# First pooling of a graph U-Net: the turned tiles use four banks of their own, and 64 skip products move behind the half turn

## The reference, cut to what matters

```python
def topk_pool(x, w, src, dst, mask, k):
    score = jnp.tanh((x * w).sum(-1) / jnp.sqrt((w * w).sum()))
    _, idx = jax.lax.top_k(score, k)
    ...
    mask2 = mask & kept[src] & kept[dst]
    return (x[idx], new_id[src], new_id[dst], mask2, idx)
...
for i in range(DEPTH):
    x = gcn_conv(x, dn_W[i], dn_b[i], src, dst, mask, n)
    x = jax.nn.relu(bn_train(x, dn_g[i], dn_beta[i]))
    xs.append(x)
    k = int(RATIO * n)
    x2, src2, dst2, mask2, idx = topk_pool(x, pool_w[i], src, dst, mask, k)
    ...
x = jax.nn.relu(gcn_conv(x, bot_W, bot_b, src, dst, mask, n))
for i in range(DEPTH):
    ...
    x = jnp.concatenate([xf, xs[DEPTH - 1 - i]], axis=1)
    x = gcn_conv(x, up_W[i], up_b[i], src, dst, mask, n)
    x = jax.nn.relu(bn_train(x, up_g[i], up_beta[i]))
```

## Time and profile before

| | |
|---|---|
| time, median of 3 runs | 1024.85 us (1023.67 to 1025.37) |
| profiled execution, span | 1043.1 us |
| mean granted TensorE clock | 0.970 |
| PE busy | 914.4 us (88%) |
| DVE busy | 593.5 us (57%) |
| ACT busy | 404.2 us (39%) |
| POOL busy | 62.9 us (6%) |
| POOL's gathers, line 832 | 20, 945 ns each |

### The profile page before, as it was taken

One profiled execution on the slowest core, in us unless ns is written; L12 is line 12 of the kernel. 1 busy time (PEld: TensorE's weight loads), 2 busy tenths in 40 slices (PEclk: granted clock), 3 DMA queues, 4 the chain that ended last, 5 costly groups with the idle time before them and its releaser, 6 DMA issues.

```text
span 1043.1 us, 17654 instructions
## 1 busy us (share of the span) xinstructions
PE 914.4 (88%) x7259; PEld 604.6 (58%) x7259; DVE 593.5 (57%) x1559; ACT 404.2 (39%) x897; POOL 62.9 (6%) x84
## 2 busy tenths in 40 slices
PE   2348999999999999999999999686988788899997
PEld 1346666876755557766475665555545445456555
DVE  5779999996937934463230265454462555525311
ACT  0889999992652001464020031555214412221200
POOL 4000000000000000000000001322002200130000
PEclk9979999999999999999999999897999699999999
DMA  5010000006920002003000004573214100151002
GB/s 161 8 28 2 2 1 2 2 2 272 401 116 1 1 1 64 1 2 125 1 1 1 1 1 121 210 221 83 92 35 134 47 1 2 34 218 67 2 1 64
DMA packets 39359, 65.86 MB, mean 63 GB/s; under 512 B 3508, under 2 KB 27293, under 8 KB 38756
## 3 DMA queue, kind: packets, MB, share of 16 engines
q1 hardware_dynamic: 34318, 45.14, 12.5%
q0 software_dynamic: 4064, 17.86, 5.3%
q10 hardware_dynamic: 886, 1.61, 0.5%
HBM read 28.29 MB, written 36.31 MB: 62 GB/s over the span
## 4 chain that ended last, share of the span: by engine, by line
PE 59%; DVE 26%; ACT 5%; DMA 3%; issue 3%; another core or an unknown queue 3%; POOL 0%; ACTq 0%; DVEq 0%; SPq 0%; POOLq 0%
PE psum L3115 25%; DVE region L1076 7%; PE psum L2497 7%; DVE region L1069 6%; PE psum L2609 6%; PE psum L2838 3%; PE psum L2574 2%; DVE region L1674 2%; PE psum L2402 2%; PE psum L2940 2%; PE psum L2427 1%; PE psum L3062 1%; PE psum L2931 1%; ACT region L2222 1%
## 5 line engine op out<-in xcount | busy, mean ns | idle before, releaser
L3115 PE MATMUL psum<-adj,region 128*128 128x448 fp8e4 (+1 forms) x1200 | 202.6, 329 | 1.1 <-DVE region L1913 1.0
L3115 PEld LDWEIGHTS psum<-adj,region 128*128 128x128 f16 x1200 | 116.5, 98 | 81.0 <-DVE region L1913 1.7
L2427 PE MATMUL psum<-region 128*128 128x200 bf16 (+2 forms) x1176 | 111.7, 230 | 26.8 <-DVE region L1076 18.5
L2427 PEld LDWEIGHTS psum<-region 128*128 128x128 bf16 x1176 | 93.7, 99 | 61.3 <-DVE region L1076 32.9
L2064 ACT ACTIVATE adj<-psum 128x400 fp8e4<-128x400 f32 x196 | 86.4, 519 | 14.9 <-PE psum L2431 14.3
L1076 DVE TENSOR_TENSOR region<-iota_key,region 128x1200 bf16<-128x1200 bf16 x147 | 91.2, 672 | 0.0
L2402 PE MATMUL psum<-adj,region 128*128 128x448 fp8e4 x350 | 90.4, 350 | 0.0
L1674 DVE CAST region<-psum 128x512 fp8e4<-128x512 f32 (+2 forms) x87 | 47.3, 597 | 75.1 <-PE psum L2931 35.5
L1069 DVE TENSOR_TENSOR region<-iota_lo,region 128x3072 bf16<-128x3072 bf16 x49 | 85.5, 1746 | 5.9 <-PE psum L2431 5.7
L2222 ACT ACTIVATE region<-psum 128x512 fp8e4<-128x512 f32 (+6 forms) x111 | 62.0, 599 | 66.5 <-PE psum L3097 20.8
L1941 DVE SCALAR_TENSOR_TENSOR region<-psum,unfit,region 128x448 f32<-128x448 f32 (+3 forms) x34 | 20.1, 622 | 109.5 <-PE psum L3115 97.3
(11 more groups left out here) (376 smaller groups left out, 1281.3 us busy)
## 6 DMA issues: line engine op xcount, KB each, us to landing
both_table<-adj SPq DMA_DIRECT2D x1, 10000.0 KB, 28.7
adj_table<-adj SPq DMA_DIRECT2D x1, 10000.0 KB, 54.7
region<-dk_dram SPq DMA_DIRECT2D x2, 1568.0 KB, 6.3
both_table<-region SPq DMA_DIRECT2D x1, 2704.0 KB, 10.9
half_table<-region SPq DMA_DIRECT2D x2, 832.0 KB, 5.2
xs_dram<-nodebuf SPq DMA_DIRECT2D x1, 1600.0 KB, 5.2
nodebuf<-xs_dram SPq DMA_DIRECT2D x1, 1600.0 KB
half_table<-region SPq DMA_DIRECT2D x2, 768.0 KB, 5.6
```

Source lines behind the costliest of these rows:

```text
L2427: pe.matmul(psum[:, q % BUILD_BANKS, i * KEYS + k0:i * KEYS + k1], hot_lo[:, r, c, j, :, i], hot_key[:, r, c, j, k0:k1, i], start=(n == 0) ...
L3115: last = pe.matmul(psum[:, b if b < BLOCKS else LAST_BANK, 0:width], here[:, t, k, :], rows, start=(t == 0 and k == 0), stop=(t == n_src - ...
```

## The change

Three things are changed in the first pooling, and one with them in the second.

- The rings are tables: at level 0 two banks for each engine, 3 and 4 for ScalarE and 5 and 7 for VectorE; at level 1 three for each as before. The place in the ring is counted from the first unit of the pooling.
- At level 0 the 64 last products of pass 0 move from before the half turn to behind it, ahead of the 50 of pass 1, and `take_skip(0)` moves on ScalarE to just before `take_skip(1)`. Units of level 0 no longer wait for `skip_out`.
- Pass 1 sums into bank 6 in place of 7. Since the degree sums stand in bank 6 too, the first of them waits for `take_skip(1)`.
- At level 1 the first unit now uses bank 0, so it waits for the first copy of `take_skip(2)`, where it waited for the second.

```diff
-TURN_BANKS = 3
+TURN_BANKS = (((3, 4), (5, 7)), ((0, 1, 2), (3, 4, 5)))
...
-        SKIP_PASSES = ((0, 0, 3, 0), (0, 3, 4, 7), (0, 4, BLOCKS, 0), (1, 0, 3, 0), (1, 3, 4, 3))
+        SKIP_PASSES = ((0, 0, 3, 0), (0, 3, 4, 6), (0, 4, BLOCKS, 0), (1, 0, 3, 0), (1, 3, 4, 3))
...
-            bank = TURN_BANKS * e + k % TURN_BANKS
+            banks = TURN_BANKS[level][e]
+            bank = banks[u // 2 % len(banks)]
...
-                        take_skip((0, 2, 3)[below])
+                        if below > 0:
+                            take_skip((0, 2, 3)[below])
                         for u in range(0, turns(below) if below < PACKINGS else 0, 2):
                             e, k, bank, to, source = turn_unit(below, u)
                             if u in (len(half_units(below)), len(half_units(below)) + 1):
                                 if below == 0:
+                                    take_skip(0)
                                     take_skip(1)
...
-                skip_sums(skips, SKIP_PICK[below][3], skip_sizes(skips))
+                if below > 0:
+                    skip_sums(skips, SKIP_PICK[below][3], skip_sizes(skips))
+
                 def sum_degrees(n):
...
-                        if below == 1:
+                        if below == 0:
+                            pe.wait_ge(skip_out, SKIP_OUT[1])
+                        else:
                             pe.wait_ge(skip_kept, SKIP_GROUPS[1])
...
                         if below == 0:
+                            skip_sums(0, SKIP_PICK[0][3], skip_sizes(0))
                             skip_sums(1, 0, skip_sizes(1))
...
-                    if k >= TURN_BANKS and e == 0:
-                        pe.wait_ge(act_turned, k - TURN_BANKS + 1)
-                    elif k >= TURN_BANKS:
-                        pe.wait_ge(dve_turned, k - TURN_BANKS + 1)
-                    if e == 0 and u // 2 < TURN_BANKS:
-                        pe.wait_ge(skip_out, (0 if below == 0 else SKIP_OUT[1]) + bank + 1)
+                    ring = len(TURN_BANKS[below][e])
+                    if u // 2 >= ring and e == 0:
+                        pe.wait_ge(act_turned, k - ring + 1)
+                    elif u // 2 >= ring:
+                        pe.wait_ge(dve_turned, k - ring + 1)
+                    if below == 1 and e == 0 and u // 2 < ring:
+                        pe.wait_ge(skip_out, SKIP_OUT[1] + bank + 1)
```

## The result

The change made the kernel slower. Its median is 1041.11 us (1036.74 to 1041.49, 4 runs) against 1025.11 us (1023.67 to 1027.32, 4 runs) before; the ratio is 1.0143, 95% interval 1.0121 to 1.0164. Timed again beside later runs, it was 1037.70 against 1024.65 (4 and 17 runs), ratio 1.0127 (1.0110 to 1.0143); so the loss is 16.0 us by the first medians and 13.1 by the second. I had forecast 1023.9 and a range up to 1027.2.

A forecast was written before the change was run, and what follows sets the result against it. It took late signals from TensorE to copying engines under gathers as the bound. First pooling -0.8 and second -0.4 sum to -1.2 us; allowing for the clock, 1024.85 - 1.0 gave 1023.9, range 1020.2 to 1027.2.

The forecast's parts named there:

- What bounds the kernel now: First pooling: signals from TensorE to a copying engine are late while gathers flow, a handoff of 7.3 us against 0.43.
- three holes in the chain: First pooling: ScalarE waits 24.88 us, TensorE 7.97 us before the half turn, and the full turn is held until 714.8.
- Half turn, -1.4 us: First pooling: 16 matmuls filled early give -1.7 us, rings of two cost +0.3; last fill from 689.51 to 688.1.
- Skip products: First pooling: 114 products take 21.9 us, until 710.0; the moved 12.3 us lie under the store and second gathers.
- Full turn, 1.13 us a tile: First pooling: 13 tiles from 712.4 at 1.13 us (bounds 1.05 and 1.20) take 14.7 us; last degree sum at 727.3.
- Clock: First pooling: TensorE at 1.2 GHz as the half turn starts, at the high level throughout the full turn.
- D: First pooling, slower: full turn starts cold and late, unit 82 at 714.0, low clock for 5.5 us; +3.2, 1028.0; chance 0.19.
- Second pooling, -0.4 us: Second pooling: first fill needs one skip copy, not two, so copies and next gathers come sooner; bounds 0 and -0.5.
- A: First pooling: with short handoffs under gathers the half turn ends 7.5 to 8.4 us earlier; time 1016.4; chance 0.12.
- wrong for me: Sign in the new profile against the forecast: half turn's copies spread over 656 to 663.

The follow-up runs named there:

- the run with dummies: The change plus 64 dummy products, whose results nothing reads, in TensorE's idle time between the picks and the half turn; 1037.40 us, ratio 1.0127.
- the half of the move: Against the change with rings of three in the full turn: 32 of the 64 products put back ahead of the half turn; 1028.71 us, ratio 1.0044.
- both parts undone: Against the change: products back ahead of the half turn and rings of three in the full turn, rings of two in the half turn alone; 1026.54 us.

## Why the prediction was wrong

**What bounds the kernel now: here it failed.** I read three holes in the chain and built on "a signal from TensorE to a copying engine is late while gathers flow". The one trace of before had them; the second trace of the same kernel has a handoff of 0.03 us under the same gathers, and no other trace of this study has such a hole. I had put the 18.2 us between span and median beside the profile and carried differences over all the same. They weren't spread over the program, as I took for granted: 19.8 us lay in the stretch on which the whole sum stood. All terms that used it, from the start of the half turn to unit 82, compared the change with a kernel that the timed runs don't show.

**Half turn, -1.4 us.** I took the start of the fills at 655 to 656 against an old start of 664.37. The clean old start is 14.3 us after the first pick (656.15), the new one 13.3 (659.14): only 1.0 us sooner, since the data are there 659.14 - 648.21 = 10.9 us after the first gather's start, which in the clean trace is 655.2, and the products end there at 655.43. The half turn then takes 25.8 us where it took 23.8: by the run with dummies (24.8) the low clock costs about 1 us and the rings of two another, where I had +0.3 for them. So it ends no sooner: the products behind it start 684.75 - 645.86 = 38.9 us after the pick, against 679.79 - 641.90 = 37.9. The term is +1.0, not -1.4.

**Skip products.** Sized right (21.7 us; I had 21.9) and placed wrongly. "The second gathers, in which TensorE turned only three tiles" was the perturbed trace. In the clean one TensorE turned tile after tile as they landed, from 691.16 - 641.90 = 49.3 us after the pick. With 114 products it can't start before 706.31 - 645.86 = 60.5. The delay is 11.2 us of the 13.6, with the half turn's 1.0 in it; the other 2.4 are the turn's own length, 79.4 - 60.5 = 18.9 us against 707.72 - 691.16 = 16.6. I had let the moved 12.3 us cost next to nothing. The run without 58 of them shows the term by time, 8.8 us, and the run with all back ahead, 9.1.

**Full turn, 1.13 us a tile.** Measured 1.41. My round of one bank was right at 1.12, but the degree sum of 0.30 stands, in the code, behind the wait for the bank and ahead of the fill, so it belongs to the round whole: 0.60 + 0.09 + 0.30 + 0.43 = 1.42. I had read the loop and not the order of its two waits. 13 x 0.28 = 3.6 us over my term. Alone it is worth less: with the products ahead the turn waits for gathers anyway, which GpSimd issues 1.25 us apart, and the rings of two cost 2.5 us (1028.61); with rings of three the move costs 6.5 us (1031.59), as a turn that starts late finds its data landed and runs at 1.05, 718.32 - 703.57 = 14.8 us in place of 16.6; both together cost 13. Each takes the cover of the other.

**Clock.** I took the high level in the full turn, and it was 1.00 there (D's fall did not come). Low in the half turn's start, as forecast.

**Second pooling, -0.4 us.** Right in mechanism: the first fill comes 0.69 us after the skip copies' start in the change's trace (792.68 - 791.99) and 0.73 in the run with this step alone, against 1.26, so 0.57 and 0.53 us sooner, just over my bound of 0.5. No time shows it (1024.13 against 1024.65, ratio 1.0000).

**The rivals.** A's mechanism is what the trace of the change shows, prompt handoffs while the gathers flow: its turn copies run on from 659.78, the very sign that I had named as wrong for me. Against the trace that I read, the pooling did get shorter, by (728.46 - 642.88) - 79.4 = 6.2 us, where A had 8. (Its 702 for the end of the products should be 703 to 704 by my own terms; nothing hangs on that.) The Trainium skill's rule (SBUF, Who interferes with whom) that DMA never contends with a compute engine agrees with the traces in what it speaks of, the engines' own work: the 64 products take 12.27 us under the gathers in both traces of the kernel before. It names no signals; but in the second trace those too are prompt, and I set a single trace against them. But A's price was wrong by its sign: with prompt signals the kernel before has them too, and no hole of 7.97 us to close. None of my rivals asked what the change costs if before is as prompt as after. Rival D had the right side for the wrong reason.

**What stays open.** Why the first profiled execution had late signals. It was told by its span, 18 us over the median; it didn't come back in thirteen further traces, so I could not test it, and whether the signals were late or the waiting engines themselves stood is open with it. Open as well are whether the loss from partly moved products has a floor, the 3.4 us between the two medians of the change, and the other half of what rings of two cost in the half turn beside VectorE's pace.

## What to carry to other kernels

Before reading a trace, hold its span against the timed runs of the same kernel: where they differ by more than the forecast effect, find the stretch in which the excess lies, or reason from what the engines would do without it. Work that stands ahead of a wait for data is free up to the wait's length; to move it behind is free only if the next wait is as long and nothing useful was done in it. When a ring of buffers gets shorter, write down everything between the wait for a buffer and its refill, in code order: all of it is in the round, and what doesn't need the buffer belongs ahead of the wait.

## What the runs showed of the hardware

Two executions of one program differed by 20 us in one stretch of 84 us with the same instructions, through handoffs of up to 7.3 us from a matmul to ScalarE, while the 64 products (12.27 us), the pace of the gathers' issue (one in 1.25 us) and ScalarE's copies (0.60 us) kept their length. In the change the granted clock was 0.63 from 648 to 649 and 0.50 from 649 to 661, TensorE having been idle from 647.3, and it cost about 1 us of a half turn of 25. It also fell after short waits: in the half of the move to 0.50 from 678 to 680, after TensorE had been busy for 1.13 of 2 us twice running (674 to 678), and with both parts undone to 0.50 from 710, after a wait of 2.20 us that ended at 707.36.
